# Expert tiles whose row loads are asked eight ahead, and a routing stage in another order

## The reference, cut to what matters

```python
# stage 1: one time step on 8 images of 128 x 128 (finite differences), then max(., 0)
x = maximum(f + dt * (-grad(A f) + 0.5 * grad2(B f)), 0)            # x: 8 x 128 x 128
# stage 2: 1,024 tokens of 128 features
h = layernorm(x) * ln_g + ln_b                     # over features
h = normalise over the 128 tokens of an image      # then times gamma plus beta, from a small
                                                   # net on the image's subject id
probs = softmax(h @ router_w)                      # 8 experts
gates, idx = top_k(probs, 2); gates /= gates.sum()
hid = relu(h @ exp_w1 + exp_b1)                    # 128 -> 512 for each expert
eout = hid @ exp_w2 + exp_b2                       # 512 -> 128
out = x + sum over the two chosen experts of gate * eout
```

## Time and profile before

| | |
|---|---|
| median of 2 runs | 210.2 us |
| the profiled execution | 211.22 us |
| its span | 209.4 us |
| TensorE matmul busy | 132.3 us (63%), 668 instructions |
| VectorE / ScalarE / GpSimd busy | 55.0 / 48.8 / 46.5 us |
| mean granted TensorE clock | 0.668 of full |
| data moved | 24.47 MB, mean 117 GB/s |

### The profile page before, as it was taken

The page is one execution under the profiler, slowest core; times in us unless marked ns, Lnnn a source line. Parts: engine busy times, 40 slices in busy tenths (PEclk is TensorE's granted clock), DMA queues, the critical chain, the costliest instruction groups (busy, mean ns, idle before and its releaser), DMA issues.

```text
span 209.4 us, 2303 instructions
## 1 busy us (share of the span) xinstructions
PE 132.3 (63%) x668; PEld 110.2 (53%) x668; DVE 55.0 (26%) x250; ACT 48.8 (23%) x145; POOL 46.5 (22%) x62
## 2 busy tenths in 40 slices
PE   7999699999304716655675658465746574686400
PEld 3987496886303615545564537454745473575300
DVE  2896673884200201100111011101110111013124
ACT  4356536135000421022202220222022202222200
POOL 4840000677720011101110111011101110112400
PEclk9999969999955785555555555555555555558965
DMA  6918999211791043134412442244224412500054
GB/s 194 341 72 191 155 191 223 87 35 37 235 385 39 0 141 115 28 127 131 131 41 105 133 138 46 96 132 138 45 89 138 131 29 100 153 0 2 0 159 142
DMA packets 17500, 24.47 MB, mean 117 GB/s; under 512 B 1879, under 2 KB 13351, under 8 KB 17488
## 3 DMA queue, kind: packets, MB, share of 16 engines
q1 hardware_dynamic: 15872, 22.54, 39.8%
q0 software_dynamic: 1184, 1.46, 2.0%
q10 hardware_dynamic: 432, 0.34, 0.7%
HBM read 18.04 MB, written 7.28 MB: 121 GB/s over the span
## 4 chain that ended last, share of the span: by engine, by line
DMA 34%; PE 32%; issue 12%; DVE 6%; POOL 6%; SPq 5%; ACT 2%; POOLq 1%; DVEq 0%
DMA rt<-rows_dram 28%; PE zt L865 15%; POOL rows_dram L501 6%; PE zt L855 4%; SPq L408 3%; DVE yg_t L1219 3%; DMA rows_dram<-h_row,row_i 2%; PE yt L846 2%; PE aux L846 2%; PE zt L677 2%; DMA sums<-sums_dram 2%; SPq L432 1%; PE zt L819 1%; PE zt L692 1%; DMA sums_dram<-yg_t,rt 1%
## 5 line engine op out<-in xcount | busy, mean ns | idle before, releaser
L669 ACT ACTIVATE hid_t<-zt,wt 128x128 f32<-128x128 f32 x84 | 24.0, 368 | 120.0 <-PE zt L855 120.0
L855 PE MATMUL zt<-xT_t,wt 128*128 128x128 f32 x168 | 39.9, 413 | 15.8 <-issue 14.9
L510 POOL DMA_INDIRECT sums_dram<-yg_t,rt x21 | 20.4, 972 | 119.0 <-DVE yg_t L1219 118.7
L855 PEld LDWEIGHTS zt<-xT_t,wt 128*128 128x128 f32 x168 | 34.8, 307 | 21.3 <-issue 21.3
L1219 DVE SCALAR_TENSOR_TENSOR yg_t<-zt,rt,b_t 128x128 f32<-128x128 f32 x21 | 7.4, 351 | 112.1 <-PE zt L865 112.1
L865 PE MATMUL zt<-wt,hid_t 128*128 128x128 f32 x168 | 36.6, 393 | 0.0
L865 PEld LDWEIGHTS zt<-wt,hid_t 128*128 128x128 f32 x168 | 34.8, 306 | 0.0
L846 PE MATMUL yt<-ident,rt 128*128 128x128 f32 x11 | 4.8, 436 | 26.6 <-DMA rt<-rows_dram 26.6
L501 POOL DMA_INDIRECT rows_dram<-h_row,row_i x16 | 16.1, 1006 | 6.0 <-issue 4.3
L846 PEld LDWEIGHTS yt<-ident,rt 128*128 128x128 f32 x11 | 1.9, 176 | 29.1 <-DMA rt<-rows_dram 17.8
L846 PE MATMUL aux<-ident,rt 128*128 128x128 f32 x10 | 4.6, 465 | 18.0 <-DMA rt<-rows_dram 18.0
(11 more groups left out here) (170 smaller groups left out, 116.4 us busy)
## 6 DMA issues: line engine op xcount, KB each, us to landing
wt<-in_exp_w_dram SPq DMA_DIRECT2D x21, 578.0 KB, 3.9
rows_dram<-spare_row SPq DMA_DIRECT2D x1, 3185.0 KB, 20.7
rt<-rows_dram SPq DMA_DIRECT2D x21, 65.0 KB, 3.5
we<-in_exp_w_dram SPq DMA_DIRECT2D x2, 578.0 KB, 6.9
sums_dram<-zeros SPq DMA_DIRECT2D x2, 512.0 KB, 15.6
sums<-sums_dram SPq DMA_DIRECT2D x8, 128.0 KB, 2.5
f<-in_x_dram SPq DMA_DIRECT2D x2, 256.0 KB, 4.0
ft<-in_x_exchanged_dram SPq DMA_DIRECT2D x2, 256.0 KB, 4.8
```

The source lines that it names most:

```text
L510: pool.indirect_dma_start(sums_dram, bass.IndirectOffsetOnAxis(ap=rt[:, n, ID_AT:ID_AT + 1].bitcast(I32), axis=0), yg_t[:, n, :], None, bo ...
L669: act.activation(hid_t[:, i % 2, c, :], z_t[i % 2][:, c * P:(c + 1) * P], ACT.Relu, bias=bias).then_inc(tile_hid, 1)
L855: last = pe.matmul(z_t[i % 2][:, c * P:(c + 1) * P], wt[:, i % W_SLOTS, c * P:(c + 1) * P], xT_t[:, i % 2, :], start=True, stop=True)
```

## The change: what it does

- **Requests.** After the five weights and the wait for the indirect stores, `rows(0)` to `rows(7)` are asked for at once. From then on the order is `weights(5), rows(8), weights(6), rows(9), ...`. What each request waits for is the same.
- **Fill.** `spare_rows` holds eight rows in each partition. GpSimd makes them at its very start with two memsets, the second of which writes the number, so that the routing constants are not needed. The table is filled by two DMAs: 48 blocks with contiguous runs of eight rows (4,160 bytes), and the last block in single rows. They are issued right behind the load of the routing constants, ahead of the load of the second dense expert's weights, which stood ahead of the fill before.
- **Routing.** On TensorE `logits(0)` goes ahead of three of the four `layer1` of half 0, and one of these goes between `norm_transposed(1)` and `ranks(0)`; `logits(1)` goes ahead of `layer1(0, 1, 0)`, and `ranks(1)` ahead of the last two `layer1` of its half. On VectorE `row_numbers(0)` goes ahead of `token_stats(1)` and `shares(0)` right behind that. On ScalarE `gate_exponent(0)` goes up by two steps.
- **End.** Four of the eight final loads are issued by ScalarE, the other four by SyncE.

```diff
+            load(we[:, 0], exp_w[ROUTED], w_in[0])
+            load(rc[:], routing, routing_in)
+            sp.wait_ge(fills_ready, 3)
+            whole = SPARE * P
+            sp.dma_start(rows_dram[0:whole].rearrange("(q p j) w -> p q (j w)", p=P, j=FILL),
+                         spare_rows[:].rearrange("p j w -> p (j w)").unsqueeze(1).broadcast_to(
+                             (P, SPARE // FILL, FILL * ROW))).then_inc(filled, 16)
+            sp.dma_start(rows_dram[whole:whole + P], spare_rows[:, 0, :]).then_inc(filled, 16)
+            for e in range(1, DENSE):
                 load(we[:, e], exp_w[ROUTED + e], w_in[e])
-                if e == 0:
-                    load(rc[:], routing, routing_in)
-            sp.wait_ge(fills_ready, 3)
-            sp.dma_start(rows_dram.rearrange("(q p) w -> p q w", p=P),
-                         spare_row[:].unsqueeze(1).broadcast_to((P, SPARE + 1, ROW))).then_inc(filled, 16)
...
-            for i in range(TILES):
+            for i in range(ROW_SLOTS):
                 tile_rows(i)
-                if i + W_SLOTS - 2 < TILES and i >= 2:
-                    tile_weights(i + W_SLOTS - 2)
+            for i in range(W_SLOTS, TILES):
+                tile_weights(i)
+                if i + ROW_SLOTS - W_SLOTS < TILES:
+                    tile_rows(i + ROW_SLOTS - W_SLOTS)
...
-            pool.memset(spare_row[:], 0.0).then_inc(fills_ready, 1)
+            pool.memset(spare_rows[:], 0.0).then_inc(fills_ready, 1)
+            pool.wait_ge(fills_ready, 1)
+            pool.memset(spare_rows[:, :, ID_AT].bitcast(I32), TOPK * T).then_inc(fills_ready, 1)
...
-            pool.wait_ge(filled, 16)
+            pool.wait_ge(filled, 32)
...
+            for i in range(max(0, TILES - ROW_SLOTS), TILES):
+                act.wait_ge(tile_out[i % ROW_SLOTS], 16 * (i // ROW_SLOTS + 1))
+            for n in range(PIECES):
+                two = slice(n * B // PIECES, (n + 1) * B // PIECES)
+                act.dma_start(sums[:, 1, two, :],
+                              sums_dram[T:TOPK * T].rearrange("(p b) d -> p b d", p=P)[:, two, :]).then_inc(
+                                  sums_in[n], 16)
...
             layer1_by_pairs()
-            for c in range(1, C):
-                layer1(0, 0, c)
             logits(0)
+            layer1(0, 0, 1)
+            layer1(0, 0, 2)
             token_rows(0)
             pe.wait_ge(xs_ready, BH)
             norm_transposed(1)
+            layer1(0, 0, 3)
             ranks(0)
...
             wait_for_h(1)
+            logits(1)
             layer1(0, 1, 0)
-            logits(1)
             token_rows(1)
-            for c in range(1, C):
-                layer1(0, 1, c)
+            layer1(0, 1, 1)
             ranks(1)
+            layer1(0, 1, 2)
+            layer1(0, 1, 3)
...
             logit_gap(0)
+            row_numbers(0)
             moved = token_stats(1)
+            shares(0)
             scale_and_shift(1, moved)
             conditioned(1)
-            row_numbers(0)
-            shares(0)
             logit_tops(1)
```

More of the change, by code:

```diff
@@ L40 @@
 ROW_SLOTS = 8
+FILL = 8
 PIECES = 4
@@ L64 @@
 PLACE_AT = BASE_AT + E
-SPARE_AT = PLACE_AT + TOPK * B
-FIRST_ROW_AT = SPARE_AT + 1
+FIRST_ROW_AT = PLACE_AT + TOPK * B
 AHEAD_AT = FIRST_ROW_AT + SPARE
@@ L101, in routing_constants @@
     out[:, PLACE_AT:PLACE_AT + TOPK * B] = place.reshape(P, TOPK * B).astype(np.int32).view(np.float32)
-    out[:, SPARE_AT] = np.full(P, TOPK * T, np.int32).view(np.float32)
     expert, block = np.divmod(np.arange(SPARE), BLOCKS)
@@ L227, in build @@
         code = sb("code", [P, 1], I32)
-        spare_row = sb("spare_row", [P, ROW])
+        spare_rows = sb("spare_rows", [P, FILL, ROW])
         zeros = sb("zeros", [P, T])
@@ L389, in _ @@
             load(pv[:], p128, p128_in)
-            for e in range(DENSE):
-                load(we[:, e], exp_w[ROUTED + e], w_in[e])
-                if e == 0:
-                    load(rc[:], routing, routing_in)
-            sp.wait_ge(fills_ready, 3)
-            sp.dma_start(rows_dram.rearrange("(q p) w -> p q w", p=P),
-                         spare_row[:].unsqueeze(1).broadcast_to((P, SPARE + 1, ROW))).then_inc(filled, 16)
+            load(we[:, 0], exp_w[ROUTED], w_in[0])
[7 more added lines that the diff above has]
+            for e in range(1, DENSE):
+                load(we[:, e], exp_w[ROUTED + e], w_in[e])
             for k in range(TOPK):
@@ L430, in _ @@
                 two = slice(n * B // PIECES, (n + 1) * B // PIECES)
[L431 to L434, removed]
+                sp.dma_start(sums[:, 0, two, :],
+                             sums_dram[0:T].rearrange("(p b) d -> p b d", p=P)[:, two, :]).then_inc(sums_in[n], 16)
             for n in range(PIECES):
@@ L482, in _ @@
             pool.wait_ge(routing_in, 16)
-            pool.wait_ge(fills_ready, 1)
-            pool.tensor_copy(spare_row[:, ID_AT:ID_AT + 1].bitcast(I32),
-                             rc[:, SPARE_AT:SPARE_AT + 1].bitcast(I32)).then_inc(fills_ready, 1)
             pool.tensor_copy(before[:], rc[:, BEFORE_AT:BEFORE_AT + P]).then_inc(before_ready, 1)
@@ L645, in _ @@
             hidden(0, 0, 3)
+            gate_exponent(0)
             inverse_sd_tokens(1)
             conditioned(1)
-            gate_exponent(0)
             hidden(0, 1, 0)
@@ L911, in _ @@
             norm_transposed(1)
+            layer1(0, 0, 3)
             ranks(0)
             pe.wait_ge(h_row_ready, TOPK)
-            for c in range(C):
+            layer2(0, 0, 0)
+            for c in range(1, C):
                 layer2(0, 0, c)
             wait_for_h(1)
+            logits(1)
             layer1(0, 1, 0)
-            logits(1)
             token_rows(1)
-            for c in range(1, C):
-                layer1(0, 1, c)
+            layer1(0, 1, 1)
             ranks(1)
+            layer1(0, 1, 2)
+            layer1(0, 1, 3)
             for c in range(C):
                 layer2(0, 1, c)
-            pe.wait_ge(w_in[1], 16)
             for e in range(1, DENSE):
+                pe.wait_ge(w_in[e], 16)
                 for n in range(HALVES):
```

## The result

The changed kernel takes 139.99 us (139.6 and 140.37), against 210.2: ratio 0.666, interval 0.658 to 0.674. The prediction was 140.0, in a range of 133 to 163. The profiled execution took 139.6 us with a span of 137.8.

The account below looks back on a forecast made before the run. Latency of a request ring, not a full engine or DMA, bounds the loop. Third tile at 69.5, plus 54.0, plus 16.5 less 0.8: span 139.2; plus 1.8 around it, less 1.0 to the median: 140.0 us, range 133 to 163.

Parts of the forecast that it names:

- The loop: Third to last tile's `layer1`: 18 tiles at 3.0 us each, 54.0 us instead of 120.4.
- The ring: In the old loop: `yg`, request, landing, transposition, `layer2`, `yg` again; a latency bound of 6.87 us a tile.
- the lower end: Lower bound for the 18 tiles of the loop: 52.7 us, beside 54.0 taken.
- The gap of 0.98 us: TensorE's idle ahead of `layer1` from `yg` and VectorE's copy, 0.79 and 0.98 us; claimed to stay.
- The clock: TensorE's clock in the loop: taken as high from the third tile on, with TensorE about 72% busy.
- alternates: Rival, 13%: pauses of 0.8 to 1.0 us a tile make the loop's clock go up and down; 156 us.
- The weights' supply: In the loop, `weights(i+1)` behind rows waiting for tile i-5's scatter: 9.3 of 12.65 us, slack 2 to 3, cost nothing.
- weights late: Rival, 7%: the loop's new scatter wait replaces the old one; 3.3 to 3.7 us a tile, 145 to 153 us.
- The front: Before the loop: earlier fill and routing; first transposition at 62.35 instead of 65.35, -3.0 us, bounds -7 and -1.
- the chain that was named: At the front: five weights keep the DMA engines busy from 53 to 62.7 us, rows queue behind; first transposition 62.35.
- The end: Eight final loads issued on two queues: -0.8 us, bounds 0 and -1.8.
- The sum: Whole kernel: front, loop and end give span 139.2, profiled execution 141.0, median 140.0 us.

Follow-up runs that it names:

- run 1: The kernel before with the new order of weight and row requests alone; 144.4 us, ratio 0.676.
- run 2: The changed kernel with each row load asked one tile further ahead than before the change, not five; 146.5 us, ratio 0.681.
- run 8: The changed kernel with four slots for weights instead of five; 145.4 us, ratio 0.687.
- run 9: The changed kernel with a VectorE memset of about 0.8 us ahead of each tile's copy from the fifth on; 154.1 us, ratio 0.738.
- run 10: The changed kernel with weights asked as each code is read, and VectorE copying tile i+2 ahead of gating tile i; rows eight ahead; 126.6 us, ratio 0.602.
- run 6: The changed kernel with the old order of routing steps on TensorE, VectorE and ScalarE; 141.1 us, ratio 0.673.
- run 7: The changed kernel with all eight final loads on SyncE's queue; 140.4 us, ratio 0.670.
- run 3: The changed kernel with only two weights asked ahead of the first rows, then two rows, weights 2 to 4, rows 2 to 7; median 141.2 us.
- run 4: The changed kernel with SyncE asking for each of the first five weights once its code is read, the other 16 codes after; 132.7 us, ratio 0.625.
- run 5: The changed kernel with the old fill, in its old place behind the second dense expert's weights; 141.9 us, ratio 0.676.

## Why the prediction was right

**The loop.** The ring that I read in one tile was the bound. With rows out of it, 18 tiles take 52.5 us; 54.0 were predicted, 52.7 by the lower end. Run 1 shows that this alone gives 32.4 of the 33.4 percent. The gap of 0.98 us came once, at the last tile, as before; the 0.76 to 0.79 of the others was the right one to take for all.

**The clock** was rightly taken as high from the third tile on. The 13% for "alternates" had a real mechanism (runs 2 and 8, each in its profiled execution), but there it took late operands, not the regular gap; run 9 shows that even twice the gap does no harm. The rule of the Trainium skill that I set beside this rival ("TensorE: Matmul & The Clock Gate", section "A second HAM failure mode: psum-queue depth-cycling") did not come true here: with a short idle in every tile the clock of the loop is 1.00.

**The weights' supply.** The term was right at nothing, but with much less to spare than the 2 to 3 us that were worked out. Scatters land after 4.3 us (median, not 3.6) and weights after 5.1 (not 3.9), so the sum is 1.2 + 4.3 + 0.6 + 5.1 = 11.2 of 4 x 2.92 + 0.65 = 12.3 us. One round of this ring in the chain, where the weights landed 0.31 us ahead of the products:

```profile
101.04 0.36 DVE yg_t L1231
...
102.22 4.62 DMA sums_dram<-yg_t,rt
...
107.56 5.50 DMA wt<-in_exp_w_dram
113.05 0.31 issue
```

The DMA engines work 0.69 x 2.92 = 2.0 us a tile, not 2.4. Only with the gap gone (run 10) does the wait for the scatter cost time; in the changed kernel it is just hidden. The rival "weights late" was mispriced: run 8's tiles, at four slots, are mostly 2.9 to 3.2 us apart and not 3.2 to 3.6, and what costs is a rare long wait.

**The front.** -3.1 us at the first transposition, -3.0 predicted, and through the chain that was named. GpSimd's start (30.4), the stores 6.4 us sooner, the codes 0.9 sooner (0.7 predicted) are as worked out. The weights ahead hold the first rows: the last of the five lands at 61.90, about 61 predicted, and the rows at 62.12. In run 6 the two are 63.17 and 63.43, although the stores had landed sooner than in the changed kernel, and in run 7 61.57 and 61.84.

What I had not seen is how close the next chain stands. The weights hold up the last store as well: it took 6.18 us, where the 15 before it took 2.2 to 3.3, and only then, at 58.05, could the rows be asked for. Run 3 took three of the five weights out of the rows' way, so that the stores were the limit, and gained only 2.1 us there; run 4 moved the weights away from the stores too and gained 5.7. This is also why the old fill costs little (run 5: 1.6 us at the first transposition, 1.9 in the times). Its last store is issued 4.3 us later and lands at 61.71, but the weights ahead, in that trace until 62.92, would have held the rows anyway; asked at 61.88, they take 1.81 us instead of 4.07.

**The end** gave 1.0 us between the two profiles, 0.8 predicted; run 7 leaves about 0.5 of it to the two queues. From the landing of the last scatter to the end it is 9.3, 9.8 and 9.8 us in three kernels with one queue (run 7, run 1 and the kernel before), and 8.8 to 9.3 in the changed kernel and runs 3 to 6. So the rest is not settled; executions differ by as much.

**The sum** hit 140.0 partly by luck: the span was 1.4 us below the predicted one (third tile 0.3 late, loop 1.5 and end 0.2 short), and the profiled execution 0.4 below the median instead of 1.0 above. That the weights' supply cost nothing was a closer thing than the 7% for "weights late" says.

## What to carry to other kernels

In a list that runs in order, ask what stands behind each waiting request: here loads with free buffers stood behind a wait that they did not share, and that made a ring of the whole loop. The right depth has two sides: deep enough for the landing, but not so deep that the request waits for a late release with others behind it (once the loop was tight, 117.4 us with six, 120.9 with five and 126.6 with eight). And put large transfers where the DMA engines idle: asked just ahead of the small store and the small loads on which all waits, they held up both, and moving them gave 7 us (run 4).

## What was not expected of the hardware

- A store of 128 rows of 520 bytes landed in 2.2 to 3.3 us ahead of the weights (15 stores of the changed kernel), in 4.4 us when issued 0.3 us ahead of five weights (run 6), and in 6.2 to 6.4 us when issued 0.1 us behind the first of five (changed kernel) or of two (run 3).
- The clock fell after a stretch with 1.60 of 3.40 us busy (run 2), and stayed through 16 tiles with 2.13 of 3.67 us busy in one of them (run 9).
- Reading 21 codes into SyncE's registers takes 12.6 us, 0.6 each; after run 4 it is what the chain of the front ends on.
